# A graph layer on one core: the second round of work put in another order

## What is computed

```python
h  = relu(layernorm(x))
hi = h @ W1[:384] + dep_emb @ W1[384:] + b1        # dep_emb looked up by adj (types 0 and 1 here)
hj = h @ W2[:384] + dep_emb @ W2[384:] + b2
relevance = sum(hi * hj, -1)                       # [64, 64] per graph
A  = softmax(where(adj != 0, relevance, -1e9))
out = x + relu((A @ h) @ gcn_w + gcn_b) @ Wo + bo
```

## Time and profile before

| | before |
|---|---|
| device time, three runs | 364.24, 365.49, 365.90 us; median 365.49 |
| profiled execution: its own time, its span | 364.34 us, 362.4 us |
| PE busy in the span | 350.7 us (97%) |
| PE's idle stretches of over 0.4 us in the changed part | 1.09, 1.10 and 2.18 us |
| ACT, DVE, POOL busy | 271.6 us (75%), 262.4 us (72%), 172.8 us (48%) |
| granted PE clock | 1.00 throughout |

### The profile page before, as it was taken

How to read it: one execution, slowest core, us unless ns; L and a number is a source line. 1 busy time by engine, 2 the same in 40 slices (tenths; PEclk the granted TensorE clock), 3 DMA queues, 4 the chain that set the end, 5 groups by cost and what they waited for, 6 DMA issues and landing times.

```text
span 362.4 us, 9435 instructions
## 1 busy us (share of the span) xinstructions
PE 350.7 (97%) x3124; PEld 217.7 (60%) x3124; DVE 262.4 (72%) x668; ACT 271.6 (75%) x577; POOL 172.8 (48%) x349
## 2 busy tenths in 40 slices
PE   7998879999999999999999999999999999999986
PEld 7764546565756566565756666565756656565753
DVE  0998698594968767695867767695867768576664
ACT  3398795978698877778698877778788777765732
POOL 2056735655627183745728183744718174670000
DMA  7993608955547393655548393655648363544053
GB/s 220 325 251 90 175 5 140 225 132 153 145 134 207 87 260 88 196 110 151 151 127 221 87 258 89 185 114 142 167 113 234 87 174 87 117 92 143 2 143 121
DMA packets 82215, 53.87 MB, mean 149 GB/s; under 512 B 45666, under 2 KB 82148, under 8 KB 82196
## 3 DMA queue, kind: packets, MB, share of 16 engines
q1 hardware_dynamic: 81488, 53.22, 56.6%
q0 software_dynamic: 64, 0.20, 0.3%
q10 hardware_dynamic: 644, 0.20, 0.2%
HBM read 17.44 MB, written 12.58 MB: 83 GB/s over the span
## 4 chain that ended last, share of the span: by engine, by line
PE 85%; DVE 7%; ACT 2%; DMA 2%; POOL 2%; issue 2%; DVEq 0%; SPq 0%; ACTq 0%; POOLq 0%
PE bank L1142 24%; PE bank L1143 23%; PE bank L1144 23%; PE bank L1242 3%; PE bank L1393 3%; PE bank L1388 3%; PE bank L1250 2%; DMA x_all<-in_L_gnn_W_w_dram 2%; DVE stats L711 1%; PE bank L1359 1%; ACT h_tok L491 1%; PE bank L1175 1%; POOL root_sq L345 1%; PE bank L1458 1%; PE bank L1460 1%
## 5 line engine op out<-in xcount | busy, mean ns | idle before, releaser
L432 POOL TENSOR_TENSOR h_parts<-h_tok,h_parts 128x1536 f16<-128x1536 f32 (+1 forms) x15 | 43.8, 2922 | 101.2 <-ACT h_parts L473 93.6
L1142 PE MATMUL bank<-gw_hi,hT 128*128 128x385 f16 x192 | 63.0, 328 | 2.2 <-DVE hg_lo L812 2.2
L1144 PE MATMUL bank<-gw_hi,hT 128*128 128x385 f16 x192 | 62.7, 327 | 0.0
L408 POOL TENSOR_TENSOR x_all<-x_all,bo_all 128x1536 f32 (+1 forms) x16 | 54.9, 3439 | 16.0 <-ACT h_tok L491 16.0
L1143 PE MATMUL bank<-gw_lo,hT 128*128 128x385 f16 x192 | 62.5, 326 | 0.0
L1142 PE MATMUL bank<-wo_hi,z_hi 128*128 128x384 f16 x180 | 58.8, 327 | 0.0
L1143 PE MATMUL bank<-wo_lo,z_hi 128*128 128x384 f16 x180 | 58.7, 326 | 0.0
L1144 PE MATMUL bank<-wo_hi,z_lo 128*128 128x384 f16 x180 | 58.7, 326 | 0.0
L1142 PE MATMUL bank<-hT,m_hi 128*128 128x512 f16 x144 | 54.6, 379 | 0.0
L1143 PE MATMUL bank<-hT,m_hi 128*128 128x512 f16 x144 | 54.6, 379 | 0.0
L1144 PE MATMUL bank<-hT,m_lo 128*128 128x512 f16 x144 | 54.6, 379 | 0.0
(11 more groups left out here) (163 smaller groups left out, 658.5 us busy)
## 6 DMA issues: line engine op xcount, KB each, us to landing
x_all<-in_x_dram SPq DMA_DIRECT2D x16, 768.0 KB, 6.1
out_dram<-x_all SPq DMA_DIRECT2D x15, 768.0 KB, 4.5
hg_parts<-hg_lo SPq DMA_DIRECT2D x32, 192.0 KB, 3.4
hg_parts<-hg_hi SPq DMA_DIRECT2D x32, 192.0 KB, 3.9
x_all<-in_L_gnn_W_w_dram SPq DMA_DIRECT2D x2, 576.0 KB, 5.2
out_dram<-x_all SPq DMA_DIRECT2D x4, 192.0 KB, 1.9
gcn_raw<-in_L_gnn_gcn_w_dram SPq DMA_DIRECT2D x1, 576.0 KB, 11.0
x_all<-in_L_gnn_Wo_w_dram SPq DMA_DIRECT2D x1, 576.0 KB, 11.6
```

The source lines that it names most:

```text
L408: nc.gpsimd.tensor_tensor(x_all[:, s, :, :], x_all[:, s, :, :], bo_all[:, :, :].broadcast_to([P, KT, D]), ALU.add).then_inc(x_biased, 1)
L432: ins = nc.gpsimd.tensor_tensor(h_parts[:, at, 1, :], h_tok[:, at, :], h_parts[:, at, 0, :], ALU.subtract)
L1142: nc.tensor.matmul(dst, lh, rh, start=(c == 0), stop=False)
L1144: last = nc.tensor.matmul(dst, ll, rh, start=False, stop=(c == DC - 1))
```

## The change

It touches the end of the first round and the second round; the loop for supertiles 2 to 15 is as it was.

- PE: T(1) goes to banks 1, 2, 3 instead of 3, 4, 5, with waits on the lo halves of G instead of on hg tiles. The fourth hg tile of supertile 0 goes to bank 7 instead of 0. The `type_row` matmul stands after the second hg tile instead of the third, and in bank 6. In `second_round` the attention's transposes stand after the second hg tile instead of the first, the third tile ahead of the aggregation, and S(1) ahead of the fourth tile.
- ACT: the type sums of the second half stand ahead of the third G chunk's read-out; one Wo split stands ahead of T(1)'s read-out, the other two and the first read-out of G(1) between the two halves of `move_scores(0)`; the first read-out of G(1) so comes ahead of the second half of the move. Z(0) and hg(1) are read in another order.
- DVE: the casts `third_high_part` leave for POOL; the order of the G and Z lo halves, Wo lo halves and statistics is changed.
- POOL: both `make_bias` stand one step earlier; it takes the four casts of supertile 2, `third_high_part`.
- SP: the second half of adj is issued ahead of x(2).

```diff
-        EARLY_BANK = (3, 4, 5)
-        FIRST_HG_BANK = (3, 4, 5, 0)
+        EARLY_BANK = ((3, 4, 5), (1, 2, 3))
+        FIRST_HG_BANK = (3, 4, 5, 7)
...
+            sp.dma_start(adj_all[:, HALF:, :], adj_rows[:, HALF:, :]).then_inc(adj_rest_loaded, 16)
             sp.wait_ge(x_loaded, 16)
             load_x(2)
-            sp.dma_start(adj_all[:, HALF:, :], adj_rows[:, HALF:, :]).then_inc(adj_rest_loaded, 16)
...
             add_bias(0)
+            make_bias(0)
             main_coefficients(1)
             pool.wait_ge(h_ready, 2 * KT * 2)
-            make_bias(0)
+            make_bias(1)
             main_coefficients(2)
-            make_bias(1)
...
-            token_low(2, range(0, HALF_TILES))
-            token_low(2, range(HALF_TILES, KT))
+            def third_high_part(k):
+
+                pool.wait_ge(third_token, k + 1)
+                nc.gpsimd.tensor_copy(h_parts[:, k, 0, :], h_tok[:, k, :]).then_inc(h_ready, 2)
+
+            for tiles in (range(0, HALF_TILES), range(HALF_TILES, KT)):
+                for k in tiles:
+                    third_high_part(k)
+                token_low(2, tiles)
...
             def second_round():
+                wo_high_part(0)
                 for c in range(DC):
                     early_high_part(1, c)
-                for c in range(DC):
-                    wo_high_part(c)
-                move_scores(0)
+                move_scores(0, range(1))
+                wo_high_part(1)
+                wo_high_part(2)
                 g_high_part(1, 0)
+                move_scores(0, range(1, GT))
                 g_whole(0)
-                exponentials(0)
                 g_high_part(1, 1)
                 g_whole(1)
+                exponentials(0)
+                g_high_part(1, 2)
+                g_whole(2)
                 third_tokens(range(0, HALF_TILES))
                 attention_out(1)
-                g_high_part(1, 2)
-                g_whole(2)
                 third_tokens(range(HALF_TILES, KT))
-                aggregated(1)
+                z_parts(0, 0, bank[Z_BANK[0]][:, :])
+                act.wait_ge(z_done, DC)
+                hg_high_part(1, 0)
+                z_parts(0, 1, bank[Z_BANK[1]][:, :])
+                z_parts(0, 2, bank[Z_BANK[2]][:, :])
+                for k in range(1, KT):
+                    hg_high_part(1, k)
...
                 g_low_part(1, 0)
+                g_low_part(1, 1)
                 wo_low_part(0)
                 attention(0, prev=False)
-                g_low_part(1, 1)
+                g_low_part(1, 2)
                 wo_low_part(1)
                 attention_high(1, prev2=False)
+                part_statistics(3, range(KT))
+                z_low_part(0, 0, bank[Z_BANK[0]][:, :])
+                rows_and_low(1, 0)
+                z_low_part(0, 1, bank[Z_BANK[1]][:, :])
                 wo_low_part(2)
-                third_high_part(0)
-                g_low_part(1, 2)
-                part_statistics(3, range(0, 2))
+                z_low_part(0, 2, bank[Z_BANK[2]][:, :])
                 for k in range(1, KT):
-                    third_high_part(k)
-                part_statistics(3, range(2, KT))
+                    rows_and_low(1, k)
...
                 free_hg_tile(1, 0, 1)
+                free_hg_tile(1, 1, 1)
                 transposed_attention(1)
-                free_hg_tile(1, 1, 1)
+                free_hg_tile(1, 2, 1)
                 aggregation(1, Z_BANK)
-                for k in range(2, KT):
-                    free_hg_tile(1, k, 1)
                 scored_supertile(1, 1)
+                free_hg_tile(1, 3, 1)
```

More of the change, by code:

```diff
@@ L205, in gnn_layer_program @@
         scores = bank[7][:, N // 2:N].rearrange("p (k j) -> p k j", k=KT)
-        early_bank = [bank[b][:, :].rearrange("p (k t) -> p k t", k=KT) for b in EARLY_BANK]
+        early_bank = [[bank[b][:, :].rearrange("p (k t) -> p k t", k=KT) for b in banks] for banks in EARLY_BANK]
         g_bank = [bank[b][:, :].rearrange("p (q i) -> p q i", i=S) for b in G_BANK]
@@ L495, in early_high_part @@
                 act.wait_ge(early_t, DC * s + c + 1)
-                nc.scalar.activation(hT_parts[s][:, :, 0, c, :], early_bank[c], ACT.Relu).then_inc(early_high, 1)
+                nc.scalar.activation(hT_parts[s][:, :, 0, c, :], early_bank[s][c], ACT.Relu).then_inc(early_high, 1)
             def gcn_high_part(c):
@@ L588, in _ @@
             types_above(2)
+            types_above(3)
             g_high_part(0, 2)
@@ L591, in _ @@
             hg_high_part(0, 0)
-            types_above(3)
+            early_normalise(1, range(0, EARLY_WIDE))
             hg_high_part(0, 1)
-            early_normalise(1, range(0, EARLY_WIDE))
             hg_high_part(0, 2)
@@ L613, in attention_out, with move_scores @@
                                      ACT.Copy).then_inc(attT_copied, 1)
-            def move_scores(s):
-                act.wait_ge(s_done, s + 1)
-                for g in range(GT):
+            def move_scores(s, pairs=range(GT)):
+                if pairs[0] == 0:
+                    act.wait_ge(s_done, s + 1)
+                for g in pairs:
                     if g:
@@ L876, in _ @@
                                     ALU.mult, ALU.mult).then_inc(weight_scales_ready, 1)
-            part_statistics(1, range(2, KT))
+            part_statistics(1, range(1, KT))
             nc.vector.tensor_scalar(out_half[:, :], unscale[:, SC_GCN:SC_GCN + 1], 1.0 / Y_SCALE, None,
@@ L908, in _ @@
             g_low_part(0, 0)
+            g_low_part(0, 1)
             statistics(2)
-            g_low_part(0, 1)
+            dve.wait_ge(type_row, 1)
+            nc.vector.tensor_reduce(type_top[:, :], bank[6][0:1, 0:4], AX.X, ALU.max).then_inc(type_step, 1)
+            dve.wait_ge(type_step, 1)
+            nc.vector.tensor_scalar(has_types[0:1, :], type_top[0:1, 0:1], 0.0, None, ALU.is_gt).then_inc(types_known, 1)
             g_low_part(0, 2)
@@ L913, in _ @@
             dve.wait_ge(pair_bias_made, 3)
[L914 to L921, removed]
+            for k in range(KT):
+                rows_and_low(0, k)
             with typed(dve):
@@ L1170, in early_transposes @@
                 for c in range(DC):
-                    if s:
-                        hg_read(c + 1)
+                    if s and c < 2:
+                        pe.wait_ge(g_split, c + 2)
+                    elif s:
+                        hg_read(1)
                     for k in range(KT):
-                        last = nc.tensor.transpose(early_bank[c][:, k, :], h_tok[:, k, c * P:(c + 1) * P], ident[:, :])
+                        last = nc.tensor.transpose(early_bank[s][c][:, k, :], h_tok[:, k, c * P:(c + 1) * P],
+                                                   ident[:, :])
                     last.then_inc(early_t, 1)
@@ L1284, in _ @@
             for k in range(KT):
-                if k == DC:
-                    pe.wait_ge(g_split, 1)
                 hg_tile(0, k, 0, gcn_ready if k == 0 else None)
-                if k == 2:
+                if k == 1:
                     pe.wait_ge(type_sums, 4)
                     pe.wait_ge(pairs_copied, 2)
-                    nc.tensor.matmul(bank[7][0:1, 0:4], ones[:, 0:1], type_sum[:, :], start=True,
+                    nc.tensor.matmul(bank[6][0:1, 0:4], ones[:, 0:1], type_sum[:, :], start=True,
                                      stop=True).then_inc(type_row, 1)
```

15 lines of the change are left out of this document (6 added, 9 removed).

## The result

| | before | changed |
|---|---|---|
| device time, seven runs | 363.84 to 366.07 us; median 365.49 | 362.15 to 362.42 us; median 362.24 |
| ratio of the times | | 0.9927, 95% interval 0.9906 to 0.9948 |
| profiled execution: its own time, its span | 364.34 us, 362.4 us | 362.20 us, 360.4 us |
| granted PE clock in the profiled execution | 1.00 | 1.00 |

The changed kernel is 0.73% faster by the ratio of the times. The medians lie 3.25 us apart (0.89%), the two profiled executions 2.1 us.

What follows compares the result with a forecast made beforehand. PE bounds the kernel, so only its holes (at most 4.4 us) can be won. Type sums 0.2 + bank 0 1.7 - output's wait 0.5 = 1.4, less 0.9 at supertile 2: 0.5 us; 365.49 - 0.5 = 365.0 us, range 363.4 to 366.8.

Steps and rivals of the forecast that it cites:

- The branch: End of first round: its 1.4 us ahead of T(1) stays; only type_row's 0.2 us wait goes, T(1) at 35.7.
- The hole in S(0): PE's 1.10 us hole behind the branch: kept in the forecast; rival that it shrinks, up to 1.1 us won, chance 0.15.
- The scatter: Runs of the kernel before, 1.7 us apart; their median's 1.15 us above the profiled execution was carried into the forecast.
- a gain of over 0.5%: Whole kernel: faster by over 0.5% needs the S(0) hole gone and the runs' scatter with it; chance 0.12.
- wait at bank 0: PE ahead of supertile 1's fourth hg tile: wait of 0.45 us instead of 2.18, 1.7 us won.
- the output's wait for z_lo: Supertile 1's output waits for Z's lo halves on DVE, costing 0.5 us; it starts at 55.55 against 56.98.
- supertile 2's new wait: PE ahead of supertile 2's first hg tile: about 1.0 us on DVE's G lo half, until 68.4; takes back 0.9.
- the gain that is left: After supertile 2's wait, 1.4 us shrinks to 0.5 us, which the PE-bound loop hands on.
- POOL's casts: Supertile 2's four casts: 0.53 us each, DVE's saving only fills idle time; slow-casts rival up to 2.2 us slower, chance 0.10.
- h of supertile 2: Lands at 60.1, PE asks at 61.4: cost nothing; late-h rival up to 2.2 us slower, slow casts 0.10.
- x(2) and the coefficients: First round: x(2) with 1.7 us slack, coefficients 0.45 us later, cost nothing; late-first-round rival 365.5 to 366, chance 0.06.
- the two engines' blocking each other: Rival, DVE and POOL in SBUF: 0.35 us of gain lost, around 365.4, up to 366.3; blocking or nothing 0.24.

Runs made afterwards that it cites:

- late_flag: Changed kernel with DVE's two has_types instructions put back among the hg lo halves; median 364.37 us, ratio 0.9989 to the kernel before.
- early_flag: Kernel before with only has_types made early, second round and banks as before; median 363.64 us, ratio 0.9961.
- before_again: Kernel before, unchanged, run to see its two groups of times; median 364.48 us, ratio 0.9996.
- hole_filled: Kernel before with nine added 512-column matmuls in the hole ahead of supertile 1's fourth hg tile; median 364.37 us, ratio 0.9977.
- sets 1 to 3: Three sets of follow-up runs, each with the kernel before taken again beside it: medians 364.66, 364.54 and 364.28 us.
- early_flag_filled: Kernel before with has_types early and nine added matmuls in the hole ahead of the fourth hg tile; median 362.90 us, ratio 0.9952.
- s1_last: Changed kernel with S(1) behind the fourth hg tile again, on PE alone; median 362.51 us, ratio 0.9936.
- casts_on_dve: Changed kernel with supertile 2's four casts back on DVE, ahead of and amid supertile 3's statistics; median 363.98 us, ratio 0.9975.
- early_flag_banks: Kernel before with has_types early, T(1) in banks 1, 2, 3 and supertile 0's fourth hg tile in bank 7; 363.68 us, ratio 0.9978.

## Why the prediction was wrong, step by step

**The branch: the failed step.** "New banks for T(1) therefore win nothing, and the load cannot move ahead of the matmuls. T(1) starts at 35.7." The first clause holds, the second doesn't. In the kernel before, the load started at 34.5 and the last matmul at 34.48, and I read that coincidence as a limit. The load had been waiting for `has_types`, which DVE finished at 34.47, among its hg lo halves. The change moved it, and the load went to 32.0 (late_flag sends it to 35.1, early_flag moves it alone). The trace of before could have told: SP, which has no matmuls, loaded the flag at 34.5 too. PE's queue passes the branch while earlier matmuls are still to run, so T(1) starts 1.42 us earlier (35.90 to 34.48), of which the forecast had 0.2. POOL passes the branch as well, at 41.1, where PE doesn't wait for it.

**The hole in S(0)** was kept "a fixed number of instructions behind the branch", and given up to 1.1 us as a rival, with a chance of 0.15. It went whole, with the same instructions between. Nor was its 1.10 us a fixed size: before_again has 0.41 and hole_filled 0.66. Four profiles with a late flag have 1.93 + 0.27, 1.09 + 1.10, 1.00 + 0.66 and 1.01 + 0.41 us, and those with an early flag neither hole. That fits something that must arrive after the branch, and is seen only when the branch is resolved late. That it is the fetch of instructions is my reading. The profile's DMA view does count four packets on its "instruction" queues from 36 to 38 us of the kernel before, but not for which engine, and no run shows the cause by itself. G(1) came at 37.82, not right behind the forecast end of S(0), 39.7, with 0.67 us of the gain already taken back by T(1)'s lo halves, which I had as late for nobody.

**The scatter.** "Runs of the kernel before lie 1.7 us apart" was taken for scatter, and the median's 1.15 us over the profiled execution was carried to the forecast. It is a second effect of the 2.18 us hole: the clock fell behind it in 33 of the 78 runs of sets 1 to 3. In the seven runs of the result four lie at 365.49 and above and three at 364.24 and below. Their clocks are not on record, but of the 78 runs the 45 at full clock took 364.82 us or less, and the 33 others 365.29 or more. So the median of before is in the group that lost its clock, and the changed kernel has no such run. The Trainium skill, TensorE: Matmul & The Clock Gate, "Part 1: The HAM clock gate", has the two levels and the fall behind idle time, and says that the moment of a change of level varies from run to run; the rows agree that there are two levels, that idle time brings the lower one, and that not every run has it. The page's rule for how much idle time it takes doesn't fit the rows, and the rows decide: holes of 1.98 to 2.18 us did it in about half of the runs. The forecast gave 0.12 to a gain of over 0.5%, with the hole and the scatter gone. That is what came, but it named no cause for either.

**The second round itself** was sized well. Forecast and found: wait at bank 0 0.45 and 0.54, the output's wait for z_lo 0.5 and 0.55, supertile 2's new wait 1.0 and 0.88, and the gain that is left 0.5 and 0.4 to 0.5 (early_flag_filled). Its gain was given back where the text put it: s1_last moves 1.2 us at bank 0, and 0.1 to 0.3 arrive. Too small was the part of POOL's casts. casts_on_dve shows 1.3 us for them, since with the casts ahead of DVE's lo halves bank 0 is late again, and the new order without their move is 0.9 us worse than the old (361.7 against 360.8 of early_flag).

**What was costed at nothing.** h of supertile 2 was never late, x(2) and the coefficients neither: PE's four waits above are all of its waits from 25 to 75 us. Of the two engines' blocking each other a little shows in the changed kernel: `wo_lo` 0.69 us at 46.84 with POOL in its casts and 0.61 at 52.53, and the pair of casts beside it 1.29 instead of 0.95. That is 0.08 us for DVE and 0.34 for POOL. Against this rival the prediction had that no row shows DVE held; casts_on_dve has one, 0.75 us behind POOL's two-input subtraction. So the direction that the Trainium skill's rule (SBUF — State Buffer, "SBUF: two separate sides") added to the traces is seen, to within 0.2 us of the whole of POOL's instruction. That it cost the changed kernel nothing more was narrow: POOL's second subtraction ended at 52.25, and the last `wo_lo` started at 52.53.

**The sum.** Span at full clock: the flag 1.1 us in set 3 and 1.6 in set 1, the second round's order with POOL's casts 0.4 to 0.5. Together that is 1.5 in set 3 (362.0 to 360.5) and 2.0 between the two profiled executions (362.4 to 360.4), of which the one of before had the longest hole in S(0). The clock is the rest of the medians' 3.25 us: 1.1 beside the profiled executions' 2.1, or 1.5 if the median of the result's three faster runs of before (363.97) is taken.

## What to carry to other kernels

When two events coincide in a trace, ask which of them waited for what before calling one the limit of the other: a flag that a branch loads should be made well ahead of the last work queued in front of the branch. When repeated runs of a kernel form two groups, look at the granted clock around PE's longest hole before calling it scatter: here a hole of 2 us cost up to 1.9 more. Where work is moved between DVE and POOL, look at what the other engine does at the same moment, not only at the idle time (casts_on_dve: 0.75 us). And a split that lets one read-out go earlier must not put a late engine's wait ahead of the softmax.

## What the runs showed of the hardware

- PE's queue resolved a branch while matmuls ahead of it in the program still had to run: load at 32.0 us, last of those matmuls at 34.31 (changed kernel). A late flag cost 1.4 to 2.2 us in two holes (1.01 + 0.41 in before_again, 1.00 + 0.66 in hole_filled, 1.09 + 1.10 before, 1.93 + 0.27 in late_flag).
- A DVE cast of 128x384 float32 took 1.10 us instead of 0.35 while POOL worked on two tensors in SBUF (casts_on_dve); POOL's own cast of that size takes 0.48 us (changed kernel).
- The clock fell behind holes of 1.98 to 2.18 us in 5 or 6 of 10 to 12 runs (before_again 5 of 12, early_flag 6 of 12, early_flag_banks 5 of 10, casts_on_dve 6 of 10), but never behind 1.74 us (s1_last, 8 runs), nor behind the 1.93 us ahead of T(1) in late_flag (12 runs). (The lengths are those of one profiled execution each.) Which runs lose it, and why the 1.93 us hole is harmless where 1.98 is not, stays open.
- In casts_on_dve the lower clock cost only 0.5 us of span (361.7 to 362.2) against 1.4 to 1.9 in the sets of before. The wait at supertile 2, which shrank to 0.28 us in its profiled execution, may have covered a part; this was not tried by itself.
